# A window-attention block on one core: probabilities times values as one 128x66 product per head, or as two 64x34 products in the two halves of the output partitions

## What is computed

```python
h = layernorm(x, norm1_g, norm1_b)             # windows: (1024, 64, 48)
q, k, v = split(hw @ qkv_w + qkv_b)            # (1024, 3 heads, 64, 16)
attn = softmax(einsum('bhnd,bhmd->bhnm', q * SCALE, k) + bias, axis=-1)
out = einsum('bhnm,bhmd->bhnd', attn, v)       # the step that is changed
x = shortcut + (out @ proj_w + proj_b)
x = x + gelu(layernorm(x, norm2_g, norm2_b) @ fc1_w + fc1_b) @ fc2_w + fc2_b
```

## Time and profile before

| | |
|---|---|
| median of 3 runs | 1255.76 us (1251.75 to 1273.67) |
| span of the profiled execution | 1264.7 us, mean granted TensorE clock 0.964 |
| TensorE / its weight loads, busy | 1142.1 / 1056.0 us |
| ScalarE, VectorE, GpSimd, busy | 955.9, 914.8, 578.5 us |

### The profile page before, as it was taken

The page is one execution under the profiler, slowest core; times in us unless marked ns, Lnnn a source line. Parts: engine busy times, 40 slices in busy tenths (PEclk is TensorE's granted clock), DMA queues, the critical chain, the costliest instruction groups (busy, mean ns, idle before and its releaser), DMA issues.

```text
span 1264.7 us, 29743 instructions
## 1 busy us (share of the span) xinstructions
PE 1142.1 (90%) x8132; PEld 1056.0 (83%) x8132; DVE 914.8 (72%) x2794; ACT 955.9 (76%) x2819; POOL 578.5 (46%) x821
## 2 busy tenths in 40 slices
PE   2999999889999999998899999998889999999997
PEld 2888888878888888887888888888888999999997
DVE  5677776777776777677777777677676777777773
ACT  2787887887887878788888878788876666667664
POOL 3334433333333343333333343233346988988982
PEclk9999998999998999899999999899989999999999
DMA  1000000000000001000000000010000111111111
GB/s 48 13 26 25 31 32 26 29 31 26 25 25 25 25 27 34 27 28 31 28 25 25 25 25 29 24 35 31 19 13 15 49 37 40 47 37 42 45 37 50
DMA packets 24744, 38.26 MB, mean 30 GB/s; under 512 B 4055, under 2 KB 20634, under 8 KB 24730
## 3 DMA queue, kind: packets, MB, share of 16 engines
q1 hardware_dynamic: 24730, 38.10, 9.5%
HBM read 25.50 MB, written 12.58 MB: 30 GB/s over the span
## 4 chain that ended last, share of the span: by engine, by line
PE 67%; ACT 25%; issue 5%; DVE 1%; POOL 1%; DMA 0%; SPq 0%; ACTq 0%; POOLq 0%
PE scores_ps L551 13%; PE mixed_ps L504 8%; PE scores_ps L487 8%; ACT k_blocks L721 6%; ACT tokens_r L709 5%; PE kv_ps L466 5%; PE probs_t_ps L494 5%; ACT v_blocks L732 4%; PE q_ps L460 4%; PE kv_ps L460 4%; PE scores_ps L483 4%; ACT tokens_t L708 3%; PE turn_ps L515 3%; ACT probs L737 3%; PE kv_ps L544 2%
## 5 line engine op out<-in xcount | busy, mean ns | idle before, releaser
L721 ACT ACTIVATE k_blocks<-kv_ps 32x128 f32<-32x128 f32 x768 | 204.8, 267 | 79.7 <-PE kv_ps L460 73.7
L504 PE MATMUL mixed_ps<-v_blocks,probs_t 128*128 128x66 f32 x1536 | 222.3, 284 | 32.7 <-ACT probs_t L714 32.7
L504 PEld LDWEIGHTS mixed_ps<-v_blocks,probs_t 128*128 128x128 f32 x1536 | 207.7, 205 | 47.5 <-issue 41.9
L487 PE MATMUL scores_ps<-k_blocks,q_blocks 96*128 96x192 f32 x1024 | 221.5, 340 | 0.0
L362 POOL TENSOR_TENSOR small<-stats 128x16 f32<-128x16 f32 x64 | 15.0, 235 | 445.0 <-DVE stats L840 445.0
L377 POOL TENSOR_TENSOR rstd<-small,minus_half 128x16 f32<-128x16 f32 x64 | 208.3, 3255 | 0.0
L954 DVE TENSOR_REDUCE row_top<-scores_ps 128x6 f32<-128x384 f32 x256 | 142.8, 558 | 83.4 <-PE scores_ps L487 78.2
L487 PEld LDWEIGHTS scores_ps<-k_blocks,q_blocks 96*128 96x128 f32 x1024 | 189.6, 201 | 0.0
L551 PEld LDWEIGHTS scores_ps<-wfc,hidden 128*128 128x128 f32 x1536 | 181.1, 192 | 5.3
L551 PE MATMUL scores_ps<-wfc,hidden 128*128 128x96 f32 x1536 | 179.9, 274 | 0.0
L958 DVE TENSOR_TENSOR lowered<-scores_ps,row_top 128x384 f32<-128x384 f32 x256 | 142.8, 558 | 11.9
(11 more groups left out here) (116 smaller groups left out, 2270.0 us busy)
## 6 DMA issues: line engine op xcount, KB each, us to landing
x_in<-in_x SPq DMA_DIRECT2D x256, 48.0 KB
x<-in_x SPq DMA_DIRECT2D x128, 96.0 KB
out<-x SPq DMA_DIRECT2D x128, 96.0 KB
pos_in<-in_L_conv_rel_bias_table SPq DMA_DIRECT2D x8, 10.6 KB
wfc_in<-in_L_conv_fc_w SPq DMA_DIRECT2D x2, 36.0 KB
wqkv_in<-in_L_conv_qkv_w SPq DMA_DIRECT2D x2, 27.0 KB
wfc<-in_L_conv_fc_w SPq DMA_DIRECT2D x2, 24.0 KB
gains<-in_L_conv_norm_g SPq DMA_DIRECT2D x2, 0.2 KB
```

The source lines that it names most:

```text
L487: mm = pe.matmul(bank[:, at:at + HEADS * TOK], q_blocks[:, k % 2, a, :, :].rearrange("p b q -> p (b q)"), k_blocks[:, k % 2, a, :, :].rear ...
L504: mm = pe.matmul(mixed_ps[:, MIX * h:MIX * h + MIX], probs_t[:, h, :], v_blocks[:, k % V_BUFS, h, :], start=True, stop=True)
L721: ins = act.activation(k_blocks[rows, k % 2, :, h, :], kv_ps[rows, at:at + 2 * TOK].rearrange("p (a t) -> p a t", a=2), ACT.Copy)
```

## The change

`v_blocks` gets an axis for the stripe half, with 34 columns (2 windows x 16 channels and 2 columns of ones) for each. For each head there are two matmuls in place of one: the 64 columns of probabilities of half b are the weights, 34 columns stream through, and the product goes to partitions 64b to 64b + 63 of `mixed_ps`. The result needed by both halves then lies in the same columns, and the normalising multiply is one instruction over 128 partitions in place of two over 64.

```diff
-MIX = 2 * 2 * HD + 2
+MIX = 2 * HD + 2
-        v_blocks = sb("v_blocks", [128, V_BUFS, HEADS, MIX])
+        v_blocks = sb("v_blocks", [128, V_BUFS, HEADS, 2, MIX])
...
                 for h in range(HEADS):
                     if h == 1:
                         wait(pe, probs_t_ok, g + 1)
-                    mm = pe.matmul(mixed_ps[:, MIX * h:MIX * h + MIX], probs_t[:, h, :], v_blocks[:, k % V_BUFS, h, :],
-                                   start=True, stop=True)
+                    for b in range(2):
+                        rows = slice(TOK * b, TOK * b + TOK)
+                        mm = pe.matmul(mixed_ps[rows, MIX * h:MIX * h + MIX], probs_t[:, h, rows],
+                                       v_blocks[:, k % V_BUFS, h, b, :], start=True, stop=True)
                 mm.then_inc(mixed_mm, 1)
...
-                        dst = v_blocks[rows, (k + m) % V_BUFS, :, 0:MIX - 2].rearrange("p h (b a d) -> p b h a d", b=2, a=2)
+                        dst = v_blocks[rows, (k + m) % V_BUFS, :, :, 0:MIX - 2].rearrange("p h b (a d) -> p b h a d", a=2)
...
-                for b in range(2):
-                    rows = slice(TOK * b, TOK * b + TOK)
-                    own = mixed[rows, :, 2 * HD * b:2 * HD * b + 2 * HD].rearrange("p h (a d) -> p h a d", a=2)
-                    ins = dve.tensor_tensor(heads[rows, k % 2, :, :, :].rearrange("p a h d -> p h a d"), own,
-                                            broadcast(inv_sum[rows, :, :], 3, HD), ALU.mult)
-                ins.then_inc(heads_ok, 1)
+                dve.tensor_tensor(heads[:, k % 2, :, :, :].rearrange("p a h d -> p h a d"),
+                                  mixed[:, :, 0:2 * HD].rearrange("p h (a d) -> p h a d", a=2),
+                                  broadcast(inv_sum[:, :, :], 3, HD), ALU.mult).then_inc(heads_ok, 1)
```

More of the change, by code:

```diff
@@ L851, in _ @@
             dve.memset(k_blocks[:, :, :, :, :], 0.0)
-            dve.memset(v_blocks[:, :, :, :], 0.0).then_inc(setup_dve, 1)
+            dve.memset(v_blocks[:, :, :, :, :], 0.0).then_inc(setup_dve, 1)
             dve.memset(tokens_t[C2:C2 + 1, :, :], 1.0)
@@ L859, in _ @@
             for a in range(2):
-                ins = dve.memset(v_blocks[TOK * a:TOK * a + TOK, :, :, MIX - 2 + a:MIX - 1 + a], 1.0)
+                ins = dve.memset(v_blocks[TOK * a:TOK * a + TOK, :, :, :, MIX - 2 + a:MIX - 1 + a], 1.0)
             ins.then_inc(blocks_zeroed, 1)
```

## The result

| | before | changed |
|---|---|---|
| median | 1260.72 us (4 runs, 1251.75 to 1273.67) | 1521.22 us (4 runs, 1518.34 to 1539.24) |
| ratio | | 1.209, 95% interval 1.199 to 1.220 |
| profiled span, mean granted clock | 1264.7 us, 0.964 | 1516.7 us, 0.748 |

What follows compares the result with a forecast made beforehand. It took TensorE, alternating with ScalarE, as the bound: 2.7 mixes x 0.29 us x 32 batches = 25 us, plus about 2 us at the lower clock, on 1255.8 gave 1283 us, range 1236 to 1310.

Steps and rivals of the forecast that it cites:

- the sum: End of the run: 2.7 full mix prices of 0.29 us a batch, x 32 = 25 us; +27 us with lower-clock mixes.
- A tenth of the time runs at the lower clock: Mixes in stretches at 1.2 GHz pay double, about 2 us more over the run.
- D: Rival inside the mix: in halves, weights no longer load under a running matmul; +190 to +500 us, 1450 to 1750; chance 0.07.
- What bounds the kernel: Batch chain alternates TensorE and ScalarE pieces; TensorE's work has a price, VectorE's savings almost none.
- Pace before: TensorE in a mix before the change: six weight loads of 0.11 us, 0.67 us, bound by loads.
- Point 1: Inside the mix: twelve half-size loads one after another, 0.056 us each, still 0.67 us; +0.00 to +0.02 us per mix.
- Point 2: Inside the mix: if both column halves run side by side, as little as 0.34 us; bounds -0.33 to +0.02 us.
- Point 3: Borders between whole and half array: matmuls run out before new weights load; way in +0.15 us, way out +0.13.
- rival A: Mixes: drains at the borders, halves side by side inside; -0.06 to +0.07 us a mix, 1251 to 1264 us; chance 0.25.
- Point 4: Normalising on VectorE: one multiply replaces two, 0.255 us less a mix, 65 us in all; costed at nothing on the end.
- Exposure of 2.7 of 8 mixes: Per batch, only 2.7 of eight mixes' full prices reach the end; idle time behind others hides theirs.
- The sign of being wrong that I had named: In the changed profile: mix starts to next group in under 0.5 us, or a load spacing over 0.1 us.

Runs made afterwards that it cites:

- 6: Changed kernel with 8, 10 and 3 superfluous matmuls filling TensorE's waits in steps 6, 7 and 3: 1246.22 us, ratio 0.979 to the kernel before.
- 10: Changed kernel with 7 and 9 superfluous matmuls in the waits of steps 6 and 7, none in step 3: 1240.36 us, ratio 0.973 to the kernel before.
- experiment 2: Kernel before with the new v_blocks layout, whole-array 68-column products, and one unused 64x34 product behind the third of each mix: 1294.52 us, ratio 1.011.
- 9: Kernel before with 7 and 9 superfluous matmuls in the waits of steps 6 and 7, none in step 3: 1240.48 us, ratio 0.973.
- 16: Changed kernel with 10 superfluous matmuls in the 1.7 us wait of step 7 only: 1248.44 us, ratio 0.990 to the kernel before.
- 13: Kernel before with only the first head's product per mix, on the whole array, from second to last-but-one batch: 1278.64 us, ratio 1.012.
- 14: Kernel before with only the first head's product in the loop's mixes, plus one unused 64x34 product behind it: 1434.92 us, ratio 1.135.
- 3: Changed kernel with quads 5, 6 and 7 of each batch as whole-array products with two multiplies: 1301.67 us, ratio 1.022 to the kernel before.
- 5: Changed kernel with two unused whole-array matmuls of 384 float32r columns ahead of each mix: 1427.94 us, no ratio given.
- 12: Changed kernel with each of the six products in halves issued twice: 1429.58 us.
- 15: Changed kernel with each of the six products in halves issued three times: 1327.20 us, ratio 1.051 to the kernel before.
- 8: Changed kernel with loops swapped, three products of half 0 and then three of half 1: 1612.05 us, ratio 1.265 to the kernel before.

## Why the prediction was wrong

**The step that failed is in the sum:** "A tenth of the time runs at the lower clock ... Mixes there pay double, about 2 us more." It priced the mixes at the lower clock and took the share of time at that clock over from the kernel before. That share went from a tenth to more than half of the front part (764 us, of some 1200), and carried everything else on TensorE with it. Filling the waits (6, 10) takes all of it away, so this is shown. No rival of mine had it; D (1450 to 1750 us) has the right time for a wrong reason, as its mechanism would lie inside the mix, and a mix takes 0.79 us at the higher clock.

**Point by point.**
- What bounds the kernel: right as far as it went. TensorE's and ScalarE's pieces alternate, and the waits were where the rows put them. What I did not ask of the earlier trace rows is how the kernel came back each time from the fall behind the 1.72 us wait, and whether the change touches that.
- Pace before (0.67 us a mix, bound by loads): right. 
- Point 1, loads in sequence: wrong. They start in pairs, 7 ns apart, and the twelve take 0.29 us to the start of the last.
- Point 2, the lower bound of 0.34 us: this happened. The Trainium skill's sentence on tiles working in parallel ("TensorEngine Tiling (Array Packing)", Tiling Modes) was the better guide than my row count of loads that had only one array to go to.
- Point 3, the drains: right in the idle time and close in size; that the last matmul runs out is my reading, which no row isolates. Way in 0.31 us between loads (62.29 to 62.60) against 0.12 before: +0.19, forecast +0.15. Way out: the last load starts at 62.60 + 0.43 - 0.13 = 62.90, the next at 63.08, 0.18 against 507.68 - (507.07 + 0.75 - 0.19) = 0.05: +0.13, as forecast, though by luck: I had 0.236 against 0.111, each some 0.06 too long.
- Points 1 to 3 together: +0.06 us a mix; rival A had -0.06 to +0.07. With the clock held this gave 1240.4 against 1240.5 us, as A says (-5 to +8). So the 25 us that the sum has for the mixes fail by themselves, clock or no clock: with 0.06 for 0.29 they would be 2.7 x 0.06 x 32 = 5. The sign of being wrong that I had named also came: from the first load of the mix to the next group are 0.48 us (62.60 to 63.08), under 0.5.
- Point 4, VectorE's 65 us hidden: right; 68 us went from its busy time, and the kernels with the clock held do not differ.
- Exposure of 2.7 of 8 mixes: too high by the one test there is. In experiment 2 the mix cost 0.44 us more and the end 14 us, that is 14 / (0.44 x 32) = 1 of 8, with an interval of 0.3 to 1.6.

**The cause in one chain.** TensorE waits 1.7 us for ScalarE's copies once a batch; at or behind this wait the clock falls to 1.2 GHz, in 19 batches before and in 22 with the change. Before, it was back after 3.4 to 10.2 us of TensorE's work behind the wait. Now every mix is over in about half the time, between two idle borders, and the clock stays down for 34 to 37.5 us. Shown: the halves cost nothing where the clock is held (9, 10), a filled wait prevents nearly all of it (16), shortness alone makes falls more frequent but brief (13), borders alone leave the clock as it was (2), both together do nearly all of it (14), whole mixes right behind the wait bring the clock back within 7 us (3), and more work in the mixes undoes it in part (5, 12) or nearly (15). Not settled: why halves one after the other lower the clock further (8), and why a mix in halves that is made as long as a whole one brings the clock back so much later (12 against 2).

## What to carry to other kernels

When an edit makes the engine that bounds the kernel do less, look at the granted clock before the sum: a stretch at the lower clock that the kernel leaves after a few microseconds is margin, and shorter work with idle borders can use it up. Fix the wait that starts the fall first; 16 superfluous matmuls a batch, in the two waits of 1.3 and 1.7 us, made either version 2.7% faster than the kernel before (9, 10), and only then can the edit itself be judged. Dividing a product over halves of the array divides the loads' time too, but pays two run-outs at its borders, so it wants long stretches between them, not six products.

## What the runs showed of the hardware that I had not expected

- Weight loads into the two column halves of the array start 7 ns apart and run side by side: 12 float32 loads of 64 columns in 0.43 us, where 6 of 128 columns take 0.75. Issued half by half they took 0.57.
- Each passage between whole and half array costs TensorE 0.13 to 0.19 us more than loads without one, at the higher clock. The way in shows as idle time of the loads with "issue" as releaser (0.19 us at 62.60); the way out hardly shows as idle time.
- TensorE can stay at the 1.2 GHz level for 34 us with matmul records over 98% of the time, and the return to 2.4 GHz at 522.9 us comes ahead of the batch's longest waits, not behind them. The Trainium skill ("TensorE: Matmul & The Clock Gate", Part 1) has sustained matmul work release the clock. The kernel before agrees; in the changed one a stream that the busy column shows as full did not release it, and more matmuls in the same stream did (0.858 in experiment 5), so the busy column does not tell when the clock will come back.
- A kernel can get slower by leaving work out (1278.64 us with two thirds of the mix left out, against 1270.28 on its chip) and faster by doing products three times over (1327.20 against 1429.58 us twice and 1521.22 once).
